# Sixteen-head attentions of a two-layer kernel: masked keys instead of masked queries, score matmuls of 32 rows and 512 columns in pairs of row strips, probability copies shared by two engines

## Chip, cores and metric

One core of a Trainium2 chip runs the whole program. The metric is the device time of one execution in microseconds (us), the median of several runs. The engines are PE (TensorE: matmuls and transposes; PEld is its weight load), DVE (VectorE), ACT (ScalarE), POOL (GpSimd) and SP (SyncE, which issues the DMAs). Every engine works through its own list of instructions in the order of the program, and waits on semaphores for the others.

## The reference

Six stages are added one after another to x, which has 4 batch elements of 128 tokens by 128 channels. Each stage reads the layer norm of x:

```python
x = x + _L0_xattn_ref(_layernorm(x), ctx_1024, ctx_1024, Wq, bq, Wk, bk, Wv, bv, Wo, bo)   # 16 heads, 2048 keys
x = x + _L0_attn_ref(_layernorm(x), ...)      # a state-space scan (conv, 16 states, gate)
x = x + _L0_ffn_ref(_layernorm(x), ...)       # quantised SwiGLU
x = x + _L1_xattn_ref(_layernorm(x), ctx_1024, Wg, bg, Wo, bo)   # gated attention, one head, 2048 keys
x = x + _L1_attn_ref(_layernorm(x), w_qkv, w_proj, b_proj, rel_bias_table)   # 16 heads, 128 keys
x = x + _L1_ffn_ref(_layernorm(x), ...)       # quantised MLP
```

The change is in the two attentions with 16 heads of 8 channels:

```python
# first: a head sees only the keys whose index, less the head's, is a multiple of 16: 128 of the 2048
scores = einsum('bhqd,bhkd->bhqk', Q, K) / sqrt(HEAD_DIM)
scores = where((kidx - hoff) % 16 != 0, -inf, scores)
out = softmax(scores) @ V            # then @ Wo.T + bo
# second: all 128 tokens are keys, and a bias by relative position is added
scores = einsum('bhqd,bhkd->bhqk', q, k) * scale + compute_bias(N, N, rel_bias_table)
```

## The kernel before

Everything between the stages stays in SBUF, with tokens or channels on the 128 partitions. `attention(ph)` is written once for each engine and called for the first (ph 0) and the second (ph 1) 16-head attention. It runs over steps t. A step w from 0 to 15 of an attention handles one batch element b = w // 4 and one group g = w % 4 of four heads, whose 32 channels are partitions 32g to 32g+31. These four steps of a batch element are called a block here.

One step goes through these operations: four score matmuls of 128 queries by 128 keys into one PSUM bank (PE); the negated row maxima (DVE, L753; in the second attention the bias is added by the same instruction, L758); four exponentials with row sums (ACT, L477); four transposes of the probabilities on PE (L1189); and the copy of the transposed probabilities to SBUF (DVE, L775). Transposes and copy of step w come two steps later (LAG = 2), in banks 3 and 4 in turn. Scores use banks 0 to 2 in turn.

Once for each block come: keys and values of the next block (ph 0: two times 16 matmuls into 32-partition column strips, from the transposed context); the placing of values for each head in `v_heads` (L698); `inv_sum`, its transpose (L1204) and its spread over channels; 16 matmuls of values and probabilities (`pv`); `o_T` (ACT, L488); the scaling `attn_T` (L784); the output projection `proj`; the addition to x (L790); and the moments, `rstd` and normalised `xn` for the next layer norm. The constants INVERSE to TURN say how many steps after its block's first step each of these stands. `turn_xn` transposes `xn` for the next stage, and CHANNELS says at which steps the state-space stage's convolution and gate matmuls stand in PE's list. `reduce_weight`, `weight_sums` and `weight_inverses` (from t = WEIGHTS) prepare the scales of the quantised weights.

To keep heads apart, `queries` (L730, L733) writes `q_heads`, four copies of the queries each masked to one head of the group, and the keys are copied by ACT (L427, L459) into `k_groups`, which is zero outside the group's 32 partitions. A score matmul thus reads all 128 partitions of both.

In the second attention `self_queries_keys` makes queries and keys of batch elements 0 to 2 at once and of element 3 later, `self_values` the values. The helper `mm` issues every matmul, at L1076. An f32 matmul shows as two MATMUL records in the trace, a transpose as one.

## Time and profile before

| | us |
|---|---|
| median of 3 runs (lowest, highest) | 281.3 (279.96, 281.42) |
| span of the profiled execution | 278.8 |
| PE busy | 209.7 (75%) |
| DVE busy | 205.7 (74%) |
| ACT busy | 151.6 (54%) |
| POOL busy | 74.6 (27%) |

The span runs from the first to the last instruction; a run's time also holds what lies around it, and differs from one execution to the next. In the trace the first 16-head attention fills the time from 15.56 us (first scores) to about 70 us. The state-space scan follows to 141 us, the SwiGLU to about 165 us, the gated attention to 208 us, and the second 16-head attention runs from 211.0 us (first scores) to 252.9 us (the addition for the last batch element). The rest is the last MLP. A record's time is from its start to its end, and records of one engine overlap, so the distance from one start to the next is often shorter than a record. "PEclk" is the granted TensorE clock as a share of full speed: 1.00 is 2.4 GHz, 0.50 is 1.2 GHz.

### The profile page before, as it was taken

How to read it: one execution, taken by the hardware profiler on the slowest of the kernel's cores; microseconds unless marked ns; L12 is line 12 of the kernel's file. 1: busy time of each engine (PE TensorE's matmuls, PEld its weight loads, DVE VectorE, ACT ScalarE, POOL GpSimd, SP SyncE). 2: the span in 40 equal slices, each digit the busy share in tenths (PEclk: the TensorE clock that was granted, in tenths of full speed). 3: DMA queues.
4: the chain of work that ended last, by engine and by line, in shares of the span. 5: the costliest groups of instructions: out<-in, count | busy, mean ns of one | idle time of the engine just before them, and what ended most of it. 6: DMA issues, size and time to landing. Idle time of an engine off the chain costs nothing.

```text
span 278.8 us, 4790 instructions
## 1 busy us (share of the span) xinstructions
PE 209.7 (75%) x1557; PEld 141.2 (51%) x1559; DVE 205.7 (74%) x585; ACT 151.6 (54%) x510; POOL 74.6 (27%) x73
## 2 busy tenths in 40 slices
PE   6896988898786977777762577999996699973313
PEld 4475877676752322222131354777785688851102
DVE  6358648873069999999957975767767499985675
ACT  4357659643685555555317773245336689853420
POOL 5013000049305777777794010000001000001000
PEclk9688999999979799999996899999999899997555
DMA  7999700068830000000000005000000000000001
GB/s 225 429 393 414 317 2 2 0 74 93 94 45 0 1 0 1 0 0 0 2 1 0 1 0 150 2 0 2 0 1 0 4 1 2 0 4 0 4 0 38
DMA packets 6745, 16.06 MB, mean 58 GB/s; under 512 B 320, under 2 KB 5056, under 8 KB 5696
## 3 DMA queue, kind: packets, MB, share of 16 engines
q1 hardware_dynamic: 6720, 15.75, 19.7%
q8 instruction: 13, 0.21, 0.3%
q14 instruction: 12, 0.10, 0.1%
HBM read 13.39 MB, written 2.35 MB: 56 GB/s over the span
## 4 chain that ended last, share of the span: by engine, by line
PE 38%; DVE 24%; POOL 13%; issue 12%; ACT 9%; DMA 2%; POOLq 0%; SPq 0%; another core or an unknown queue 0%; DVEq 0%; ACTq 0%
PE bank L1076 31%; POOL region L392 13%; ACT probs L477 3%; PE bank L1416 3%; DVE region L775 2%; DVE region L758 2%; DMA ctx_T_sb<-ctx_T 2%; PE bank L1189 2%; DVE neg_max L753 1%; DVE xn L685 1%; DVE stats L680 1%; PE bank L1093 1%; DVE ext L1040 1%; DVE ext L1041 1%; DVE v_heads L698 1%
## 5 line engine op out<-in xcount | busy, mean ns | idle before, releaser
L1076 PE MATMUL bank<-region,early_sb 128*128 128x512 f32 x64 | 36.8, 661 | 11.8 <-POOL region L392 11.6
L392 POOL TENSOR_TENSOR region<-region 128x512 f32<-128x512 f32 x32 | 40.5, 1268 | 14.5 <-DVE region L900 14.5
L900 DVE TENSOR_TENSOR_SCAN region<-region,bank 128x512 f32<-128x512 f32 x32 | 38.7, 1211 | 0.0
L1076 PE MATMUL bank<-k_groups,region 128*128 128x128 f32 x256 | 35.7, 285 | 1.2 <-ACT k_groups L459 1.2
L1076 PEld LDWEIGHTS bank<-k_groups,region 128*128 128x128 f32 x256 | 32.2, 198 | 3.2 <-ACT k_groups L459 1.8
L361 POOL TENSOR_TENSOR xb<-x,rows_sb 128x512 f32<-128x512 f32 x3 | 3.8, 1261 | 101.0 <-DVE x L790 43.2
L477 ACT ACTIVATE probs<-bank,neg_max 128x128 f32<-128x128 f32 x64 | 22.6, 367 | 12.9 <-DVE neg_max L753 12.5
L1076 PE MATMUL bank<-ctx_T_sb,region 128*32 128x128 f32 (+1 forms) x288 | 26.8, 345 | 3.4 <-DMA ctx_T_sb<-ctx_T 2.2
L477 ACT ACTIVATE probs<-region,neg_max 128x128 f32<-128x128 f32 x64 | 24.9, 390 | 5.7 <-DVE neg_max L758 5.5
L1076 PEld LDWEIGHTS bank<-region,early_sb 128*128 128x128 f32 x64 | 10.1, 195 | 33.2 <-POOL region L392 32.6
L775 DVE COPY region<-bank 128x512 f32<-128x512 f32 x32 | 21.8, 682 | 5.6 <-PE bank L1189 5.6
L411 ACT ACTIVATE lnv<-mv,eps_col 128x1 f32<-128x1 f32 x24 | 7.0, 291 | 33.7 <-DVE mv L681 33.6
L542 ACT ACTIVATE region<-bank 128x512 f32<-128x512 f32 x16 | 9.5, 595 | 24.2 <-POOL region L392 24.2
L1189 PE MATMUL bank<-early_sb,probs 128*128 128x128 f32 x128 | 20.7, 287 | 1.5 <-ACT probs L477 1.5
L884 DVE TENSOR_TENSOR bank<-region,bank 128x512 f32<-128x512 f32 x32 | 21.6, 676 | 0.0
L556 ACT ACTIVATE region<-region,a_neg 128x508 f32<-128x508 f32 x32 | 21.1, 708 | 0.0
L758 DVE CUSTOM_DVE_ANT_0 region<-bank,region 128x128 f32<-128x128 f32 x64 | 14.5, 282 | 5.7 <-PE bank L1076 5.7
L1189 PEld LDWEIGHTS bank<-early_sb,probs 128*128 128x128 f32 x128 | 15.2, 146 | 3.5 <-ACT probs L477 2.1
L1007 DVE COPY region<-bank 128x512 f32<-128x512 f32 x16 | 10.9, 686 | 8.1 <-PE bank L1416 8.1
L1076 PEld LDWEIGHTS bank<-region,ctx_sb 128*128 128x128 f32 x128 | 15.4, 192 | 2.9 <-issue 2.9
L1076 PEld LDWEIGHTS bank<-ctx_T_sb,region 128*32 128x32 f32 (+1 forms) x288 | 12.6, 132 | 7.7 <-issue 4.5
L1076 PE MATMUL bank<-region,ctx_sb 128*128 128x128 f32 x128 | 15.6, 275 | 0.0
(198 smaller groups left out, 410.1 us busy)
## 6 DMA issues: line engine op xcount, KB each, us to landing
ctx_sb<-ctx SPq DMA_DIRECT2D x4, 1024.0 KB, 24.5
ctx_T_sb<-ctx_T SPq DMA_DIRECT2D x3, 1024.0 KB, 10.5
late_sb<-late SPq DMA_DIRECT2D x1, 2416.0 KB, 18.4
bias_scratch<-bias_vec SPq DMA_DIRECT2D x1, 2040.0 KB, 24.7
ctx_T_sb<-ctx_T SPq DMA_DIRECT2D x2, 512.0 KB, 6.2
region<-bias_scratch SPq DMA_DIRECT2D x1, 1024.0 KB, 5.7
early_sb<-early SPq DMA_DIRECT2D x1, 512.0 KB, 3.7
region<-taps SPq DMA_DIRECT2D x1, 512.0 KB, 18.9
```

Source lines behind the costliest of these rows:

```text
L392: done(pool.tensor_tensor(read[:, k % 3, :], state[:, k % 3, :], c_sb[:, n % 2, :], ALU.mult), "read")
L477: ins = act.activation(probs[:, w % 4, j, :], src[:, j, :], ACT.Exp, bias=neg_max[:, w % 4, j:j + 1], scale=1.0 if ph == 0 else -1.0, accu ...
L542: done(act.activation(c_sb[:, n % 2, :], bank[2][:, :], ACT.Copy), "c_sb")
L556: done(act.activation(dst, src, ACT.Exp, scale=a_neg[:, hf, n:n + 1]), "decay")
L758: ins = dve.tensor_tensor_reduce(neg_biased[:, t % 3, j, :], src[:, j, :], rel_bias[:, HG * g + j, :], -1.0, HIGHEST, ALU.add, ALU.min, ne ...
L775: done(dve.tensor_copy(probs_T[:, w % (2 * NG)].rearrange("p h k -> p (h k)"), bank[3 + w % 2][:, :]), "probs_T_sb")
L884: done(dve.tensor_tensor(bank[3 + k % 3][:, :], du[:, hf, :], bank[n % 2][:, :], ALU.mult), "drive")
L900: done(dve.tensor_tensor_scan(state[:, k % 3, :], decay[:, k % NDA, :], bank[3 + k % 3][:, :], 0.0, ALU.mult, ALU.add), "state")
L1007: done(dve.tensor_copy(p2_T[:, w % 4].rearrange("p c q -> p (c q)"), bank[4 + w % 2][:, :]), "p2T_sb")
L1076: return pe.matmul(dst, lhsT, rhs, start=start, stop=stop)
L1189: ins = pe.transpose(bank[3 + w % 2][:, j * P:j * P + P], probs[:, w % 4, j, :], ident)
L1416: ins = pe.transpose(bank[4 + w % 2][:, c * P:c * P + P], p2[:, b % 2, g, c * P:c * P + P], ident)
```

## The change

The mask moves from the queries to the keys. `q_sb` holds the queries once (scaled by 8 ** -0.5), and `k_exp[:, b, j, :]` holds the keys of a batch element four times, each with only the channels of head j of every group. A score step is then one matmul of 32 partitions (a row strip of TensorE) by 512 columns. Steps are issued in pairs, (t+2, t+3) at every even t, two row strips into two of four banks. Keys of the first attention come from the 16 matmuls with `wz` without accumulation, into four column ranges of bank 6, and DVE adds the masked bias; in the second, four matmuls with `wkz` (the key weights masked for each head, made by POOL) and one ACT copy. All transposes go to bank 4, one step after the exponentials; DVE copies the even steps and ACT the odd ones. The stages of a block come two to four steps earlier, and the convolution matmuls stand elsewhere.

```diff
-LAG = 2
-INVERSE, INVERSE_T, VALUES, SCALE, PROJECT, ADD, RSTD, NORM, TURN = 6, 7, 8, 9, 10, 11, 11, 12, 13
+INVERSE, INVERSE_T, VALUES, HEADS_OUT, SCALE, PROJECT, ADD, RSTD, NORM = 4, 5, 5, 6, 7, 7, 8, 8, 9
+STEPS = 23
-WEIGHTS = 9
-LAST_TURN, LAST_QK = 2, 6
-CHANNELS = {17: [(0, 0)], 18: [(0, 1)], 23: [(0, "gates"), (1, "gates")], 25: [(1, 0), (1, 1)]}
+WEIGHTS = 6
+LAST_TURN, LAST_QK = 2, 3
+TURNS = {13: 0, 15: 1, 18: 2, 22: 3}
+CHANNELS = {16: [(0, 0), (0, 1)], 17: [(0, "gates")], 19: [(1, 0), (1, 1), (1, "gates")]}
...
+            for j in range(HG):
+                done(pool.tensor_copy(wkz[:, j, :, j, :],
+                                      L("wqkvT")[:, D:2 * D].rearrange("p (g k d) -> p g k d", g=NG, k=HG)[:, :, j, :]),
+                     "wkz")
...
             def self_keys(b):
-                act.wait_ge(S["kv_ps"], 2 * NB + 1 + b // (NB - 1))
-                for g in range(NG):
-                    rows = slice(32 * g, 32 * g + 32)
-                    ins = act.activation(k_groups[rows, g, b * P:b * P + P], bank[6][rows, b * P:b * P + P], ACT.Copy)
-                done(ins, "k_sb")
+                act.wait_ge(S["k_ps"], NB + b + 1)
+                done(act.activation(k_exp[:, b, :, :].rearrange("p j k -> p (j k)"), bank[6][:, :], ACT.Copy), "k_sb")
+
+            def turned_probs(w):
+                act.wait_ge(S["probs_T_ps"], w + 1)
+                if w // NG >= 2:
+                    act.wait_ge(S["pv"], w // NG - 1)
+                done(act.activation(probs_T[:, w % (2 * NG)].rearrange("p h k -> p (h k)"), bank[4][:, :], ACT.Copy),
+                     "probs_T_sb")
...
+                    if 0 <= t - 1 < 4 * NB and (t - 1) % 2:
+                        turned_probs(ph * 16 + t - 1)
...
+            def keys(v):
+
+                dve.wait_ge(S["k_ps"], v + 1)
+                done(dve.tensor_tensor(k_exp[:, v, :, :], bank[6][:, :].rearrange("p (j k) -> p j k", j=HG),
+                                       bk_heads[:, :, None].to_broadcast([P, HG, P]), ALU.add), "k_sb")
...
+                maxima(ph, 0)
+                for t in range(STEPS):
+                    if ph == 0 and ahead(t, 1) is not None:
+                        keys(ahead(t, 1))
+                    if t + 1 < 4 * NB:
+                        maxima(ph, t + 1)
+                    if 0 <= t - 1 < 4 * NB and (t - 1) % 2 == 0:
+                        w = ph * 16 + t - 1
                         dve.wait_ge(S["probs_T_ps"], w + 1)
...
+            def score(ph, t):
+                b, g = t // NG, t % NG
+                rows = slice(32 * g, 32 * g + 32)
+                pe.wait_ge(S["k_sb"], ph * NB + b + 1)
+                pe.wait_ge(S["q_sb"], 1 if ph == 0 else 2 + b // (NB - 1))
+                if t >= 4:
+
+                    pe.wait_ge(S["probs" if ph == 0 else "neg_max"], ph * 16 + t - 3)
+                done(mm(bank[t % 4][:, :], q_sb[rows, b * P:b * P + P],
+                        k_exp[rows, b, :, :].rearrange("p j k -> p (j k)")), "scores")
...
+                score(ph, 0)
+                score(ph, 1)
+                for t in range(STEPS):
+                    if t % 2 == 0 and t + 2 < 4 * NB:
+                        score(ph, t + 2)
+                        score(ph, t + 3)
+                    if ahead(t, 0) is not None:
+                        (keys if ph == 0 else self_keys)(ahead(t, 0))
+                    if ph == 0 and ahead(t, 1) is not None:
+                        values(ahead(t, 1))
+                    if 0 <= t - 1 < 4 * NB:
+                        w = ph * 16 + t - 1
+                        pe.wait_ge(S["probs"], w + 1)
+                        if w >= 1:
+                            pe.wait_ge(S["probs_T_sb"], w)
...
-                            ins = pe.transpose(bank[3 + w % 2][:, j * P:j * P + P], probs[:, w % 4, j, :], ident)
+                            ins = pe.transpose(bank[4][:, j * P:j * P + P], probs[:, w % 4, j, :], ident)
...
                     if ph == 1 and t == LAST_QK:
-                        self_queries_keys(NB - 1, NB)
-                    if ph == 1 and t == LAST_TURN + 1:
+                        self_queries(NB - 1, NB)
                         self_values()
```

`ahead(t, phase)` is the batch element b from 1 to 3 for which t = 4(b-1) + phase.

How PE's list changes in the first attention, where `L1076` and `L1101` are `mm`, `L1189` and `L1243` the transposes of probabilities, `ctx_T_sb` the keys or values of the next batch element and `v_heads` the `pv` matmuls. Before, from the scores of step 10 on:

```order
L1076 MATMUL bank2<-k_groups,region 128x128 x4
L1189 MATMUL bank4<-early_sb,probs 128x128 x4
L1117 MATMUL bank6<-early_sb,v_T 128x128
L1204 MATMUL bank7<-early_sb,inv_sum 16x128
L1076 MATMUL bank0<-k_groups,region 128x128 x4
L1189 MATMUL bank3<-early_sb,probs 128x128 x4
L1076 MATMUL bank5<-region,v_heads 32x128 x16
L1076 MATMUL bank7<-inv_T,cols_sb 128x128
```

And now, from the pair of steps 10 and 11 on:

```order
L1101 MATMUL bank2<-k_exp,region 128x512
L1101 MATMUL bank3<-k_exp,region 128x512
L1101 MATMUL bank6<-ctx_T_sb,region 32x128 x16
L1243 MATMUL bank4<-early_sb,probs 128x128 x4
L1101 MATMUL bank5<-ctx_T_sb,region 32x128 x16
L1243 MATMUL bank4<-early_sb,probs 128x128 x4
L1254 MATMUL bank7<-early_sb,inv_sum 16x128
L1101 MATMUL bank5<-region,v_heads 32x128 x16
L1101 MATMUL bank7<-inv_T,cols_sb 128x128
L1101 MATMUL bank0<-k_exp,region 128x512
L1101 MATMUL bank1<-k_exp,region 128x512
```

Eight score matmuls of two steps became two, keys and values stand around one set of transposes, and `pv` stands three steps earlier, ahead of the next pair of scores.

How ACT's list changes in the second attention, from the copy of the keys of batch element 2 on. Before:

```order
L459 ACTIVATE k_groups<-bank6 32x128 x4
L477 ACTIVATE probs,row_sum<-region,neg_max 128x128 x12
L459 ACTIVATE k_groups<-bank6 32x128 x4
L477 ACTIVATE probs,row_sum<-region,neg_max 128x128 x4
L488 ACTIVATE o_T<-bank5 128x128
L477 ACTIVATE probs,row_sum<-region,neg_max 128x128 x12
```

And now (`L472` is the copy of transposed probabilities):

```order
L466 ACTIVATE k_exp<-bank6 128x512
L490 ACTIVATE probs,row_sum<-region,neg_max 128x128 x8
L472 ACTIVATE region<-bank4 128x512
L503 ACTIVATE o_T<-bank5 128x128
L490 ACTIVATE probs,row_sum<-region,neg_max 128x128 x8
L472 ACTIVATE region<-bank4 128x512
L430 ACTIVATE lnv<-mv,eps_col 128x1
L431 ACTIVATE rstd<-lnv 128x1
L466 ACTIVATE k_exp<-bank6 128x512
L490 ACTIVATE probs,row_sum<-region,neg_max 128x128 x8
```

After every second step's exponentials ACT has a copy of 512 columns, and the four key copies of a batch element became one.

## Rows read from the trace of the kernel before

**Rows 1.** The page: chain of work that ended last, share of the span by line.

```profile
PE bank L1076 31%; POOL region L392 13%; ACT probs L477 3%; PE bank L1416 3%; DVE region L775 2%; DVE region L758 2%; DMA ctx_T_sb<-ctx_T 2%; PE bank L1189 2%; DVE neg_max L753 1%; DVE xn L685 1%; DVE stats L680 1%; PE bank L1093 1%; DVE ext L1040 1%; DVE ext L1041 1%; DVE v_heads L698 1%
```

**Rows 2.** Busy us (instructions) of each engine by stretch; granted clock; DMA share, GB/s.

```profile
40.00:50.00 10.00, 8.83 (x120) 7.74 (x119) 7.84 (x21) 6.58 (x32) 0.00 (x0) 1.00 0.01 2
237.00:247.00 10.00, 9.13 (x118) 7.90 (x121) 9.83 (x57) 9.28 (x48) 0.00 (x0) 1.00 0.00 0
```

**Rows 3.** PE's timeline, first attention: start, us to the last end, operation, shape, count.

```profile
15.56 1.06 PE L1076 MATMUL bank<-k_groups,region 128*128 128x128 f32 x8
...
31.63 1.06 PE L1076 MATMUL bank<-k_groups,region 128*128 128x128 f32 x8
32.53 0.60 PE L1189 MATMUL bank<-early_sb,probs 128*128 128x128 f32 x4
...
36.96 1.08 PE L1076 MATMUL bank<-ctx_T_sb,region 128*32 128x128 f32 x32
37.97 0.66 PE L1189 MATMUL bank<-early_sb,probs 128*128 128x128 f32 x4
38.56 1.08 PE L1076 MATMUL bank<-region,v_heads 128*32 128x128 f32 x32
39.57 0.48 PE L1076 MATMUL bank<-inv_T,cols_sb 16*128 16x128 f32 x2
```

**Rows 4.** The chain in order of time: a 512-column f32 matmul of the gated attention.

```profile
174.74 0.86 PE bank L1076 x2
```

**Rows 5.** Groups by shape, 9 to 70 us: count, busy us, mean ns, idle before.

```profile
L477 ACT ACTIVATE probs<-bank,neg_max 128x128 f32<-128x128 f32 x64 | 22.6, 367 | 12.9 <-DVE neg_max L753 12.5
L753 DVE TENSOR_REDUCE neg_max<-bank 128x4 f32<-128x512 f32 x16 | 10.9, 684 | 5.2 <-PE bank L1076 5.0
L775 DVE COPY region<-bank 128x512 f32<-128x512 f32 x16 | 10.9, 682 | 5.6 <-PE bank L1189 5.6
L427 ACT ACTIVATE k_groups<-bank,cols_sb 32x128 f32<-32x128 f32 x16 | 5.7, 355 | 0.2
L730 DVE TENSOR_SCALAR region<-bank,cols_sb 128x128 f32<-128x128 f32 x16 | 5.4, 402 | 4.7 <-PE bank L1076 4.7
```

**Rows 6.** The page: an ACT copy of 512 columns out of PSUM, in the scan.

```profile
L542 ACT ACTIVATE region<-bank 128x512 f32<-128x512 f32 x16 | 9.5, 595 | 24.2 <-POOL region L392 24.2
```

**Rows 7.** Busy time and granted clock, as rows 2, around two slow stretches.

```profile
22.40:25.70 3.30, 1.44 (x11) 1.09 (x9) 3.30 (x9) 3.16 (x17) 1.14 (x2) 1.00 1.03 431
25.80:29.10 3.30, 2.76 (x36) 2.28 (x37) 1.08 (x6) 1.50 (x8) 1.53 (x3) 0.50 1.00 420
217.00:220.20 3.20, 0.76 (x7) 0.68 (x7) 2.14 (x11) 3.14 (x16) 0.00 (x0) 1.00 0.00 0
220.40:223.60 3.20, 3.20 (x17) 3.20 (x17) 0.94 (x9) 0.61 (x4) 0.00 (x0) 0.50 0.01 3
```

**Rows 8.** ACT's and PE's timelines: last exponentials and last convolution, first attention.

```profile
57.37 0.37 ACT L477 ACTIVATE probs<-bank,neg_max 128x128 f32<-128x128 f32 x1 [1.02 <-DVE neg_max L753]
...
58.41 0.37 ACT L477 ACTIVATE probs<-bank,neg_max 128x128 f32<-128x128 f32 x1
...
68.91 0.20 ACT L412 ACTIVATE rstd<-lnv 128x1 f32<-128x1 f32 x1
...
69.73 3.75 PE L1076 MATMUL bank<-region 128*128 128x128 f32 x32
```

**Rows 9.** ACT's and DVE's timelines: last exponentials and last addition, second attention.

```profile
245.34 0.40 ACT L477 ACTIVATE probs<-region,neg_max 128x128 f32<-128x128 f32 x1
...
246.51 0.39 ACT L477 ACTIVATE probs<-region,neg_max 128x128 f32<-128x128 f32 x1
...
252.90 0.29 DVE L790 TENSOR_TENSOR x<-bank,xb 128x128 f32<-128x128 f32 x1 [0.58 <-PE bank L1076]
```

More of the change, by code:

```diff
@@ L1154, in self_queries_keys, with self_keys @@
                 if b0:
[L1156 to L1157 removed]
+                    pe.wait_ge(S["q_sb"], 2)
                 done(mm(bank[5][:, cols], L("wqkvT")[:, 0:D], xn_T[:, cols]), "q_ps")
[L1159 removed]
+            def self_keys(b):
+                pe.wait_ge(S["xnT_sb"], 3 * NB + b + 1)
+                pe.wait_ge(S["wkz"], HG)
+                if b:
+                    pe.wait_ge(S["k_sb"], NB + b)
+                for j in range(HG):
+                    ins = mm(bank[6][:, j * P:j * P + P], wkz[:, j].rearrange("p g k d -> p (g k d)"),
+                             xn_T[:, b * P:b * P + P])
+                done(ins, "k_ps")
             def self_values():
```

246 lines of the change are left out of this document (119 added, 127 removed).

## The prediction

> **What bounds the kernel now.** I read the chain of waits first. Its largest share, 31%, lies on PE's matmuls of `mm` [rows 1], which stand for several stages, so I read the busy time by stretch next, for the two stages that change. In the first attention PE is busy 8.83 of 10 us, DVE 7.84 and ACT 6.58: PE's list is nearly full [rows 2]. In the second DVE is busy 9.83 of 10 us and ACT 9.28, PE 9.13: all three are full and DVE leads [rows 2]. So a microsecond taken from PE counts in the first attention, and one taken from DVE in the second, until ACT is the bound, which has only half a microsecond in ten to give there. Everything from the scan to the gated attention is unchanged and starts when the first attention ends; the last MLP starts when the second ends. The sum is therefore the shift of two ends.
>
> **Prices.** Four score matmuls of 128 columns take PE 0.90 us (31.63 to 32.53) [rows 3]. One f32 matmul of 512 columns takes 0.86 us by itself [rows 4]. So a step alone gains nothing; the gain is that two row strips run side by side. No row here shows row strips. The nearest is the column strips: 32 records of 128 columns in 1.01 us (36.96 to 37.97), 32 ns each, where records of the full array take 0.90/8 = 113 ns [rows 3]. Side by side a pair costs 0.86 us, one after another 1.72. I take the first, being the nearest row in kind. Changing between full array and strips costs about 0.15 us: transposes take 0.44 us before a like shape, but 0.59 ahead of `v_heads` (37.97 to 38.56) [rows 3]. Half of it shows for a pair, so I use 0.95 us for a pair against 1.80 before.
>
> The Trainium skill (TensorE: Matmul & The Clock Gate, Part 3, packing small matmuls) gives a speed-up of 3.07 for four row strips of 512 columns, short of 4; by that a pair would be an estimated 1.1 us, and ten pairs on the path would add 1.5 us to the sum. The same skill (TensorEngine Tiling, Tiling Modes) says that a change of tiling mode drains TensorE, which speaks against this change, for it makes 16 more such switches in each direction; the trace agrees with a drain, with the 0.15 us above.
>
> DVE loses eight copies of 0.60 us start to start (0.68 each by itself) in each attention, and in the first also 16 masked queries (402 ns) for one pass over 512 columns, and gains four key additions of about 0.68 [rows 5]. ACT loses 16 key copies of 355 ns in the first attention [rows 5] and gains eight probability copies. A 512-column ACT copy out of PSUM is 595 ns [rows 6], about 0.50 when the next follows at once. The exponentials of a step keep ACT for 1.39 us in the first attention (57.37 to 58.41 is three of four) [rows 8] and for 1.56 in the second [rows 9].
>
> **First attention.** The first scores stand behind the transpose of the values as before, at 15.5 us [rows 3]; the smaller `q_sb` write is hidden there. Then a block repeats. I count from the end of the exponentials of step 4b-1:
>
> - PE: pair 0.95, keys 1.01, transposes of step 4b-1 landing after 0.66 [rows 3]: 2.6 us. ACT had finished the next exponentials at 1.4 and waits 1.2 us for this copy. That is a new wait: keys are queued ahead of the transposes.
> - PE goes on: values to 3.4, transposes 4b to 3.9, `inv_sum` 0.1, `pv` 1.01, spread 0.41, the next pair 0.95, transposes 4b+1 landing: 7.0.
> - ACT: copy 0.5, `v_T` and `o_T` 0.5, exponentials 4b+3 1.5: 9.5. About nine hand-overs of 0.04 us make it 9.85 us.
>
> Before, 15 steps passed from 15.56 to 57.37, 2.79 each, 11.1 us for a block [rows 3, 8]. Now the start-up to the end of exponentials 3 takes 8.7 us: two pairs and the keys 2.9, key addition and maxima 1.4, exponentials 2 1.4, then the wait for transposes 1, copy 0.5, `v_T` 0.3 and exponentials 3 1.5. Two blocks take 19.7. The last, without keys and values but with the weight sums, takes 8.2. The exponentials of step 15 then start at 52.1, 5.2 us earlier.
>
> The tail gives some back. The convolution of the first two batch elements (3.7 us) stands ahead of the last `pv`, as before. But half of the 3.75 us of last convolutions [rows 8], with its gates 2.3 us, now stands ahead of the last projection instead of behind it. I get the last `rstd` at 65.2 where it ended at 69.1 [rows 8], 3.9 earlier; the work behind it is shorter by the moved part, but ACT needs its table load and the activations of the others first. What reaches the scan is **-4.1 us**. POOL's quantised weights come earlier and are not waited for; its `wkz` copies (about 0.6 us) stand ahead of `w_tap`, which is used 25 us later.
>
> **Second attention.** Score matmuls wait only for DVE's maxima here, so a pair is issued early. But the copies of odd steps now stand in ACT's list, the one with least room. Its work up to the exponentials of step 15: 15 steps of 1.55 is 23.3, seven copies 3.5, three key copies 1.5, `xn_T` and `o_T` 0.8, two `rstd` 1.0, in all 30.1 us. From 212.8, where the first exponentials start (0.35 earlier than before through the shorter key copy), that gives 242.9 with no wait at all. ACT will wait, though: for transposes 3, behind the late queries, values and a pair (1.1 us); for transposes 5, behind `pv`, which waits for the 16 value placements on DVE (2.5 us); for transposes 7, behind a projection, a pair and keys (1.2 us); and 0.3 for transposes 11. So step 15 starts at 248.0, against 245.34 [rows 9]: 2.6 later. The shorter lags save 2.0 behind it: from the start of step 15 to the last addition were 7.56 us [rows 9], and are now 1.7 for the exponentials, 0.65 and 0.6 for transposes and copy, and 2.6 from `pv` on. Net **+0.6 us**.
>
> **The clock.** The granted clock fell to 0.50 for 3.3 us after PE had been busy 1.44 of 3.30 us, and once more after 0.76 of 3.20 [rows 7]. Both prices above are at 1.00. The new first attention has the same kind of thin stretch at about 21.7 to 24.2 us (1.0 us busy or less), the second at about 214 to 218.6 (2.0 of 5). Right behind each stand a pair, keys and transposes that ACT waits for, so a slow stretch costs up to 1.7 us. I count one of two: **+1.7 us**.
>
> **The sum** is -4.1 + 0.6 + 1.7 = -1.8 us on a span of 278.8, so 277.0. The profiled span lies 2.5 us under the median, 281.3, and I leave that distance: **279.5 us**.
>
> **Rivals.**
>
> 1. *The two strips of a pair run one after another.* For it: no row shows two row strips together, and each f32 matmul is two passes. Against: the column strips, whose f32 matmuls are two passes too. Price 0.86 us for every pair that the path passes. It passes about five of eight in each attention, so +8.6 us, 288.1. Half an overlap (1.29 for a pair) gives 283.8. It is slower than before as soon as a pair costs over 1.15 us.
> 2. *The clock falls in most blocks.* PE's blocks get emptier: between transposes 4b+1 and the next pair it has 0.8 us of work in 2.8. Two more slow stretches on the path add 3.4 us: 282.9.
> 3. *ACT is the bound in the first attention as well, and the waits for transposes disappear.* If PE runs ahead of my list, ACT needs 5.6 + 1.0 + 0.5 + 0.5 = 7.6 us for a block instead of 9.85. Two blocks and half the waits of the second attention give 4.5 us more: 275.0.
> 4. *The moved copies only change places:* DVE's gain is ACT's loss and the end stays. With a first attention that gains 2 and a second that loses 2 it is 281.3.
>
> **How the numbers follow.** Chances: the forecast 0.50 (276 to 282 with its clock and half a microsecond for each hand-over sum), rival 1 0.20, rival 2 0.13, rival 3 0.09, rival 4 0.08. The range 275.5 to 287 leaves out most of a full rival 1 and the lower end of rival 3. A measurement of this kernel tells about 0.5% from no change, 279.9 to 282.7. Faster than that: 0.35 of the forecast's 0.50, all of rival 3, together 0.44. Within: 0.12 of the forecast, rival 4, half of rival 2: 0.25. Slower: rival 1, half of rival 2, the rest: 0.31.
>
> **What would show it.** In the profile of the changed kernel: the two score matmuls of a pair start within some 10 ns and the pair's last end is 1.0 us behind its start (rival 1: 1.3 or 1.8). ACT's idle time ahead of the copies of odd steps is released by PE's transposes, over 1 us in each block of the first attention. The exponentials of step 15 start near 52 and 248 us less the shift of the first attention. In the second attention DVE is no longer full and ACT is the busiest. The granted clock has at most three slow stretches in both. I would be wrong from the start if the first scores came late, for the 512-column key addition now stands between keys and scores, or if the step from one block to the next were under 9 us.

## The result, and the profile after

The changed kernel takes **307.7 us** (median of 4 runs, 306.9 to 308.0) where the kernel before takes 280.95 (4 runs, 279.96 to 281.42): a ratio of **1.095, 95% interval 1.092 to 1.098**. The forecast was 279.5 us with a range up to 287. It was wrong in sign and by far in size. The profiled execution spans 306.1 us against 278.8, and its mean granted clock is 0.788 against 0.907. Ratios, here and below, leave out executions over 1.5% above the fastest of their kernel; medians and ranges hold all.

Nearly all of the 27.3 us lies in the two attentions. From the first scores to the last addition, or `rstd`, of each, the windows view of the changed kernel gives (columns as in [rows 2]: length, then busy us and instructions of PE, PEld, DVE, ACT, POOL, then the granted clock):

```profile
15.40:79.00 63.60, 55.09 (x489) 36.04 (x489) 29.36 (x81) 30.96 (x154) 17.02 (x18) 0.73 0.57 148
221.20:280.30 59.10, 46.22 (x279) 29.10 (x279) 28.36 (x184) 32.87 (x150) 0.00 (x0) 0.62 0.00 1
```

And the same two of the kernel before:

```profile
15.60:68.90 53.30, 45.99 (x570) 38.82 (x569) 36.13 (x98) 32.12 (x159) 13.09 (x13) 0.97 0.52 158
211.00:252.90 41.90, 35.05 (x353) 30.48 (x353) 34.76 (x202) 31.48 (x151) 0.00 (x0) 0.96 0.01 2
```

Three things are to be seen. The stages grew by 10.3 and 17.2 us. PE has 81 and 74 instructions fewer and is busy 9 and 11 us longer. And the clock, which was at full speed but for one short stretch in each stage, is now 0.73 and 0.62 in the mean. DVE lost 6.8 and 6.4 us of work; ACT's stayed within 1.4.

The page of the changed kernel, waits for the turned probabilities first (DVE's copy L788, ACT's copy L472), then the scores:

```profile
L788 DVE COPY region<-bank 128x512 f32<-128x512 f32 x16 | 11.1, 691 | 30.8 <-PE bank L1243 30.8
L472 ACT ACTIVATE region<-bank 128x512 f32<-128x512 f32 x16 | 9.5, 597 | 38.0 <-PE bank L1243 38.0
L1101 PE MATMUL bank<-k_exp,region 32*128 32x512 f32 x64 | 25.2, 882 | 0.7 <-ACT k_exp L466 0.7
```

Both engines that were to share the copies stand idle for PE's transposes, 30.8 and 38.0 us over the two attentions. Before, DVE's copies waited 5.6 us in the first [rows 5] and 0.1 in the second. The chain of waits still has PE's `mm` at the top, 33% of the span after 31% [rows 1]:

```profile
PE bank L1101 33%; POOL region L411 13%; PE bank L1243 7%; PE bank L1471 2%; ACT region L472 2%; ACT probs L490 2%; DVE ext L1065 1%; DVE ext L1066 1%; DVE xn L697 1%; DVE region L972 1%; DVE stats L692 1%; DVE region L1080 1%; DVE h_abs L941 1%; DVE attn_T L804 1%; ACT region L595 1%
```

The transposes (L1243, 7% where L1189 had 2%) rose most. One block of the first attention in PE's timeline, at full clock:

```profile
44.42 1.08 PE L1101 MATMUL bank<-region,v_heads 128*32 128x128 f32 x32
45.61 0.48 PE L1101 MATMUL bank<-inv_T,cols_sb 16*128 16x128 f32 x2
45.84 1.12 PE L1101 MATMUL bank<-k_exp,region 32*128 32x512 f32 x4
46.89 0.66 PE L1243 MATMUL bank<-early_sb,probs 128*128 128x128 f32 x4
48.32 0.63 PE L1243 MATMUL bank<-early_sb,probs 128*128 128x128 f32 x4 [0.78 <-ACT region L472]
49.93 0.71 PE L1101 MATMUL bank<-cols_sb,attn_T 128*128 128x128 f32 x2 [0.98 <-DVE attn_T L804]
```

A pair of score matmuls (four records, since each f32 matmul is two) keeps PE for 1.05 us, 45.84 to 46.89. So the two strips do run side by side. But behind them come gaps, and then the clock falls. The windows view around three of the slow stretches:

```profile
33.00:36.30 3.30, 1.67 (x11) 0.84 (x8) 1.67 (x5) 2.22 (x11) 0.00 (x0) 1.00 0.11 45
36.40:43.20 6.80, 6.77 (x63) 4.07 (x67) 4.26 (x13) 2.27 (x12) 0.00 (x0) 0.50 0.01 4
46.70:49.90 3.20, 1.47 (x10) 0.84 (x8) 2.12 (x5) 2.32 (x12) 0.00 (x0) 1.00 0.00 0
50.00:60.00 10.00, 9.73 (x58) 5.64 (x59) 5.44 (x20) 3.77 (x19) 3.48 (x3) 0.50 0.50 56
247.00:258.00 11.00, 9.24 (x58) 6.10 (x59) 5.85 (x34) 6.29 (x31) 0.00 (x0) 0.50 0.01 2
```

From 50 to 60 us PE is the engine that all others wait for (9.73 of 10 us busy) and runs at 1.2 GHz. ACT's timeline in that stretch shows the price, one wait of 4 us ahead of a copy:

```profile
55.35 0.60 ACT L472 ACTIVATE region<-bank 128x512 f32<-128x512 f32 x1 [3.96 <-PE bank L1243]
```

**A first estimate of the clock's share.** With only two levels of clock, a mean clock c over a span s means (1 - c)/0.5 x s at half clock: 130 us in the changed kernel, 52 before, other stages included. So 78 us more at half clock go with 27.3 us more of span, 0.35 us for each. Whether that is cause or by-product is what the experiments are for.

### The profile page after: what moved, and what is told of

It reads as the page before. It is cut to its first block, busy times and chain, and to the rows that moved or that the text cites. A ratio compares the mean times of both kernels' runs of the same rounds, so it can differ in the third digit from the quotient of the medians.

```text
span 306.1 us, 4414 instructions
## 1 busy us (share of the span) xinstructions
PE 231.1 (75%) x1393; PEld 137.8 (45%) x1395; DVE 190.6 (62%) x544; ACT 150.1 (49%) x498; POOL 75.9 (25%) x78
## 4 chain that ended last, share of the span: by engine, by line
PE 43%; POOL 13%; DVE 13%; issue 9%; ACT 8%; POOLq 0%; another core or an unknown queue 0%; DVEq 0%; ACTq 0%
PE bank L1101 33%; POOL region L411 13%; PE bank L1243 7%; PE bank L1471 2%; ACT region L472 2%; ACT probs L490 2%; DVE ext L1065 1%; DVE ext L1066 1%; DVE xn L697 1%; DVE region L972 1%; DVE stats L692 1%; DVE region L1080 1%; DVE h_abs L941 1%; DVE attn_T L804 1%; ACT region L595 1%
## 5 line engine op out<-in xcount | busy, mean ns | idle before, releaser
L1101 PE MATMUL bank<-region,early_sb 128*128 128x512 f32 x64 | 35.9, 643 | 11.7 <-POOL region L411 11.6
L1243 PE MATMUL bank<-early_sb,probs 128*128 128x128 f32 x128 | 28.7, 365 | 11.6 <-ACT region L472 10.0
L1243 PEld LDWEIGHTS bank<-early_sb,probs 128*128 128x128 f32 x128 | 19.5, 185 | 25.2 <-issue 16.9
L1101 PE MATMUL bank<-ctx_T_sb,region 128*32 128x128 f32 (+1 forms) x288 | 28.8, 387 | 2.3 <-DMA ctx_T_sb<-ctx_T 1.9
L788 DVE COPY region<-bank 128x512 f32<-128x512 f32 x16 | 11.1, 691 | 30.8 <-PE bank L1243 30.8
L472 ACT ACTIVATE region<-bank 128x512 f32<-128x512 f32 x16 | 9.5, 597 | 38.0 <-PE bank L1243 38.0
L376 POOL TENSOR_TENSOR xb<-x,rows_sb 128x512 f32<-128x512 f32 x2 | 2.5, 1264 | 101.5 <-DVE x L812 60.2
L1101 PE MATMUL bank<-k_exp,region 32*128 32x512 f32 x64 | 25.2, 882 | 0.7 <-ACT k_exp L466 0.7
L1101 PEld LDWEIGHTS bank<-region,early_sb 128*128 128x128 f32 x64 | 9.6, 188 | 33.4 <-POOL region L411 33.1
L554 ACT ACTIVATE region<-bank 128x512 f32<-128x512 f32 x16 | 9.5, 595 | 24.2 <-POOL region L411 24.2
L1101 PEld LDWEIGHTS bank<-ctx_T_sb,region 128*32 128x32 f32 (+1 forms) x288 | 14.5, 152 | 10.7 <-issue 8.8
L1101 PEld LDWEIGHTS bank<-region,ctx_sb 128*128 128x128 f32 x128 | 15.4, 192 | 2.9 <-issue 2.9
L1032 DVE COPY region<-bank 128x512 f32<-128x512 f32 x16 | 10.9, 685 | 8.1 <-PE bank L1471 8.1
L1101 PE MATMUL bank<-region 128*128 128x128 f32 (+2 forms) x52 | 14.8, 459 | 1.2 <-ACT region L438 1.2
## 6 DMA issues: line engine op xcount, KB each, us to landing
ctx_T_sb<-ctx_T SPq DMA_DIRECT2D x3, 1024.0 KB, 10.3
region<-taps SPq DMA_DIRECT2D x1, 512.0 KB, 20.3
```

What stands on the lines that cost most here:

```text
L472: done(act.activation(probs_T[:, w % (2 * NG)].rearrange("p h k -> p (h k)"), bank[4][:, :], ACT.Copy), "probs_T_sb")
L554: done(act.activation(c_sb[:, n % 2, :], bank[2][:, :], ACT.Copy), "c_sb")
L788: done(dve.tensor_copy(probs_T[:, w % (2 * NG)].rearrange("p h k -> p (h k)"), bank[4][:, :]), "probs_T_sb")
L1032: done(dve.tensor_copy(p2_T[:, w % 4].rearrange("p c q -> p (c q)"), bank[4 + w % 2][:, :]), "p2T_sb")
L1101: return pe.matmul(dst, lhsT, rhs, start=start, stop=stop)
L1243: ins = pe.transpose(bank[4][:, j * P:j * P + P], probs[:, w % 4, j, :], ident)
```

## The experiments

The theories: **A**, the halved clock takes the time, and waits matter only because they let it fall. **B**, the new waits take it themselves (one bank for transposes, ScalarE's copies behind its exponentials, keys ahead of transposes), the clock is a by-product. And on why the clock falls: **C**, matmuls on 32 rows hold it up less than matmuls on 128, whatever PE's busy time says; **D**, only idle time counts.

| kernel | median us | range (runs) | ratio to before (95%) | clock |
|---|---|---|---|---|
| changed | 307.7 | 306.9-308.0 (4) | 1.095 (1.092-1.098) | 0.788 |
| e1_fill | 287.4 | 285.6-288.3 (4) | 1.019 (1.013-1.026) | 0.883 |
| e2_all_rows | 301.2 | 300.7-302.2 (4) | 1.069 (1.064-1.075) | 0.866 |
| e3_before_strips | 299.8 | 299.2-304.8 (4) | 1.063 (1.057-1.070) | 0.828 |
| e4_keys_behind | 292.4 | 290.5-301.5 (4) | 1.034 (1.025-1.043) | 0.842 |
| e5_fill_behind | 286.7 | 284.3-288.1 (4) | 1.023 (1.010-1.035) | 0.891 |
| e6_dve_copies | 292.8 | 291.9-293.3 (4) | 1.046 (1.037-1.054) | 0.905 |
| e7_before_fill | 280.8 | 279.9-283.2 (10) | 1.004 (1.000-1.009) | 0.918 |
| e8_thin_fill | 292.5 | 289.8-304.3 (4) | 1.042 (1.030-1.053) | 0.878 |
| e9_fill_small | 282.2 | 279.7-285.4 (10) | 1.008 (1.003-1.014) | 0.904 |
| e10_fill_project | 291.1 | 284.9-294.4 (4) | too scattered for one | 0.868 |
| e11_all_rows_behind | 296.5 | 294.8-299.2 (4) | 1.057 (1.049-1.065) | 0.880 |
| e12_thin_small | 301.3 | 289.1-304.9 (6) | too scattered for one | 0.869 |

The clock is the mean of the profiled execution. The kernel before had 280.5 to 281.4 us beside them.

**Idle time filled.** e1_fill adds bf16 matmuls of 128 rows by 256 columns, with a result that nobody reads. `keep_warm(n, at)` issues n of them into bank `at`; FILL_A is 6, FILL_B is 8. Such matmuls are called fillers here:

```diff
                         pe.wait_ge(S["probs"], w + 1)
+                        if t % 2 and t < 4 * NB:
+                            keep_warm(FILL_A, (t - 1) % 4)
                         if w >= 1:
...
                         v = ph * NB + due(t, PROJECT)
+                        if t < 4 * NB:
+                            keep_warm(FILL_B, (t - 1) % 4)
                         pe.wait_ge(S["attn"], v + 1)
```

> The changed kernel with idle-time matmuls added on TensorE in both attentions: 6 bf16 products of 128 rows ahead of the transposes of odd steps (behind the wait on the probabilities) and 8 ahead of each projection's wait, into a score bank that is free. Their results are overwritten; nothing else changes. Theory A (most of the loss is the halved clock, and the waits are only what lets it fall): the mean granted clock of both attentions goes from about 0.6 to over 0.95 and the time falls from 307.7 to about 280-286 us, although PE has more to do. Theory B (the new dependency waits cost the time themselves, the clock is a by-product): the clock may rise, but the time stays over 300 us, or rises.

287.4 us, 20.3 us less although PE got more to do: 1.4 above theory A's band, 13 below theory B's. Theory B is out as the main cause, since no dependency was removed. The first attention of e1_fill, as above, is back at its old clock, the second nearly so:

```profile
15.40:69.60 54.20, 50.05 (x562) 35.36 (x561) 29.09 (x81) 31.43 (x156) 17.07 (x18) 0.97 0.65 171
213.20:260.50 47.30, 40.82 (x351) 27.54 (x351) 27.77 (x184) 32.89 (x150) 0.00 (x0) 0.92 0.01 2
```

**Rows, in the changed kernel.** e2_all_rows leaves out the separation of the four groups, so its result is not the reference's; it is there for its time:

```diff
-                b, g = t // NG, t % NG
-                rows = slice(32 * g, 32 * g + 32)
+                b = t // NG
+                rows = slice(0, P)
```

> The changed kernel with its score matmuls over all 128 partitions instead of the group's 32. The scores then sum over all four groups (this changes the computation), the number of instructions, their order and all waits stay. The two matmuls of a pair can then no longer run side by side: a pair takes about 1.72 us instead of about 1.05 at full clock, 5 us more of PE's work in each attention. Theory C (the clock falls because 32-row strips use a quarter or half of the array): the clock falls in fewer stretches and the time is lower than the changed kernel's 307.7, about 288-298 us, though PE has more work. Theory D (the clock falls for idle gaps alone, whatever the rows): idle gaps shrink by 0.7 us a pair, clock changes little, and the time is 307 to 316 us. Clearly lower than 300 us is C's, over 307 is D's.

301.2 us, between the two bands: 6.5 us faster than with strips, although pairs can't overlap any more. A pair now takes 1.82 us at full clock (37.24 to 39.06), 0.77 more than two strips, some 12 us for 16 pairs. Its clock, 0.866, means 50 us less at half clock, an estimated 18 us at the 0.37 found below; the difference is near what was measured. The sign is C's, the size is under what I gave it. By itself the run doesn't exclude D, for the longer pairs also fill gaps.

**Rows, in the kernel before.** e3_before_strips keeps everything of the kernel before and narrows its scores to the 32 rows that hold data:

```diff
-                                     q_heads[:, j, b * P:b * P + P], k_groups[:, g, b * P:b * P + P])
+                                     q_heads[32 * g:32 * g + 32, j, b * P:b * P + P],
+                                     k_groups[32 * g:32 * g + 32, g, b * P:b * P + P])
```

> The kernel before with one edit: each score matmul reads only the group's 32 partitions (the left-out ones are zero, so nothing else changes); still four matmuls of 128 columns a step, still in the same place and order. Theory C (thin rows let the clock fall): the granted clock of the first attention (15.5 to 69 us), which has been 1.00 but for one stretch, falls to 0.50 in several stretches, and the time rises from 281 to 286-300 us. Theory D (idle gaps alone): PE's busy time in microseconds and its gaps stay as they were, the clock too, and the time is within 0.5% of 281.

**299.8 us, 6.3% slower, from rows alone.** It is the cleanest run of the study: same list, same order, same waits, and the same data but for zeros. Both kernels lose their clock near 25 us. With full rows it is back after 3.3 us [rows 7]; with strips it stays down for 10.3 us in which PE has no gap. Then a stretch in which PE is busy 3.08 of 3.40 us is followed by half clock, and from 222.6 the clock stays down for 27 us:

```profile
24.60:34.90 10.30, 10.30 (x92) 8.23 (x92) 4.26 (x12) 5.12 (x26) 2.78 (x4) 0.50 0.83 343
34.90:38.30 3.40, 3.08 (x23) 2.43 (x22) 2.54 (x6) 2.01 (x11) 0.00 (x0) 1.00 0.01 2
38.30:45.10 6.80, 6.71 (x70) 5.20 (x74) 2.47 (x8) 2.87 (x16) 0.00 (x0) 0.50 0.01 2
222.60:249.90 27.30, 26.06 (x135) 21.35 (x131) 17.45 (x109) 18.00 (x85) 0.00 (x0) 0.50 0.01 2
```

What PE did in the second of these, by its timeline (15 of the 23 records are 32-row scores):

```profile
34.70 1.02 PE L1076 MATMUL bank<-k_groups,region 32*128 32x128 f32 x7
35.65 0.66 PE L1190 MATMUL bank<-early_sb,probs 128*128 128x128 f32 x4
36.24 1.15 PE L1076 MATMUL bank<-k_groups,region 32*128 32x128 f32 x8
37.32 0.66 PE L1190 MATMUL bank<-early_sb,probs 128*128 128x128 f32 x4
```

The kernel before has a stretch with much less work, all on 128 rows but for two small records, and keeps its clock behind it:

```profile
49.60:53.00 3.40, 2.17 (x20) 1.84 (x16) 3.40 (x8) 2.75 (x16) 0.00 (x0) 1.00 0.00 0
53.00:56.40 3.40, 3.40 (x28) 2.83 (x28) 2.49 (x8) 2.10 (x12) 0.00 (x0) 1.00 0.01 2
```

Theory D can't have both.

A rival has to be weighed: changing between the full array and strips costs PE time too. At full clock a step's scores and transposes take 1.67 us here (47.57 to 49.24) and 1.33 before (32.53 to 33.86). But the exponentials of steps 10 to 13 start 7.04 us apart in both kernels (50.37 to 57.41 here, 44.89 to 51.93 before), each at full clock, so in the first attention that time is hidden. In the second, steps 10 to 15 take 9.92 us at full clock against 9.34, which for a whole attention would be an estimated 2 of the 18 us. So most of the loss came through the clock.

**The order of PE's list.** e4_keys_behind moves four lines of `attention` behind the transposes:

```diff
-                    if ahead(t, 0) is not None:
-                        (keys if ph == 0 else self_keys)(ahead(t, 0))
-                    if ph == 0 and ahead(t, 1) is not None:
-                        values(ahead(t, 1))
                     if 0 <= t - 1 < 4 * NB:
...
                         done(ins, "probs_T_ps")
+                    if ahead(t, 0) is not None:
+                        (keys if ph == 0 else self_keys)(ahead(t, 0))
+                    if ph == 0 and ahead(t, 1) is not None:
+                        values(ahead(t, 1))
```

> The changed kernel with the matmuls of keys and values (512 and 128 columns) moved on PE from ahead of a step's transposes to behind them, so that ScalarE's copy of the turned probabilities and the exponentials behind it wait less. Theory B (the order of PE's list and the waits it makes cost the time): three blocks of each attention lose about 1 us each, some 5 us in all, 302 us or less. Theory A (the halved clock costs the time): the same work at the same clock with the gap in another place, 305 to 310 us; a large move in either direction only where the clock's slow stretches move too.

292.4 us, three times what B gave it, and the clock rose to 0.842 (one of the four executions took 301.5 us, at 0.809). By the expectation's last clause that is a move of the slow stretches: half clock falls from 130 to 92 us, 38 less for 15.4 us of span. Which of the two it was, the next run tells.

**Both edits.** e5_fill_behind has the edits of e1 and e4.

> The changed kernel with both earlier edits: the idle-time matmuls (6 ahead of the transposes of odd steps, 8 ahead of each projection's wait) and the matmuls of keys and values behind a step's transposes. If halved clock and wait order are two causes that add, each takes what the other leaves: the clock is at 1.00 in nearly all of both attentions, and the blocks lose another 0.5 to 1 us each on top of the 287.4 us of the fillers alone: 279-284 us. If moving the keys helped only because it filled a thin stretch (clock 0.84 instead of 0.79), there is nothing left for it to give at full clock: 286-289 us.

286.7 us, within the scatter of e1's 287.4. Beside these fillers the order of keys and transposes is worth under a microsecond, so nearly all of its 15 us in e4 came through the clock. But PE was now full of fillers, which can hide a shorter wait; no run has small groups in the first order. A group of six stands between two groups of transposes and keeps PE for 0.85 us, 43.90 to 44.75:

```profile
43.41 0.66 PE L1243 MATMUL bank<-early_sb,probs 128*128 128x128 f32 x4
43.90 0.82 PE L1103 MATMUL bank<-ones 128*128 128x256 bf16 x6
44.75 0.33 PE L1243 MATMUL bank<-early_sb,probs 128*128 128x128 f32 x1
```

**ScalarE's half of the copies.** e6_dve_copies undoes it on top of e5:

```diff
                 act.wait_ge(S["vT_ps"], v + 1)
+                if v >= 2:
+                    act.wait_ge(S["pv"], v - 1)
...
-                    if 0 <= t - 1 < 4 * NB and (t - 1) % 2:
-                        turned_probs(ph * 16 + t - 1)
...
-                    if 0 <= t - 1 < 4 * NB and (t - 1) % 2 == 0:
+                    if 0 <= t - 1 < 4 * NB:
```

> The kernel with both of those edits, and with all copies of the turned probabilities on VectorE again, none on ScalarE (one wait on pv is added for ScalarE's copy of the values, for the bank it reads). It undoes the change's last part at a clock that is held up. If the ScalarE copies are a cost (they stand behind a step's exponentials, in the list of the engine with least room), it is 2-4 us faster than the kernel with both edits; if VectorE is the one that needed relief (9.83 of 10 us busy in the second attention before), it is 2-5 us slower. My own forecast: first attention a little faster, second slower, within 1.5 us in all.

292.8 us, 6.1 slower than e5. The clock is not the reason: from 216 to 252 us in e5 and from 219 to 255 in e6 it is 0.91, in the first attentions 0.97. (The higher mean of the profiled execution, 0.905, comes mostly from the first 15 us.) My own forecast, within 1.5 us, missed. Sharing the copies is the part of the change that pays, in this order of work.

**Fillers in the kernel before.** e7_before_fill:

```diff
                     if ph == 0 and t % NG == 3 and t // NG + 1 < NB:
+                        if t == 3:
+                            keep_warm(12, (t - 2) % 3)
                         turn_values(t // NG + 1)
...
                     if ph == 1 and t == LAST_QK:
+                        keep_warm(18, (t - 2) % 3)
                         self_queries_keys(NB - 1, NB)
```

> The kernel before with idle-time matmuls in two places where TensorE waits ahead of a slow stretch: 12 ahead of the first transpose of the values in the first attention (22.6 to 24.2 us), 18 ahead of the late queries of the second (217.1 to 219.5 us). Theory A (half clock costs in proportion to PE's work on the path): both slow stretches of 3.4 us go and the time falls by 1 to 2.5 us, to 279-280 us. If the waits hide the half clock: within 0.3% of before.

280.8 us, a ratio of 1.004 (1.000 to 1.009): no gain. But the run tests less than it was meant to. The slow stretch of the first attention is gone; that of the second came all the same:

```profile
218.40:221.70 3.30, 0.85 (x7) 0.61 (x6) 2.38 (x13) 3.23 (x16) 0.00 (x0) 0.99 0.00 0
221.80:225.10 3.30, 3.30 (x17) 3.30 (x17) 0.52 (x5) 0.84 (x5) 0.00 (x0) 0.50 0.01 2
```

The 18 fillers stand in the wrong place. PE's wait in the first row is 2.45 us ahead of the values (`self_values`, 221.17). The late queries, with the fillers ahead of them, come at t = 6, and the fillers run from 227.79 to 229.76, behind the slow stretch and where PE had no wait. So one short stretch was removed and 2 us of work was added elsewhere. What a single short stretch costs stays open.

**Fillers on 32 rows.** e8_thin_fill is e1_fill with the same number, place and columns of fillers:

```diff
+            def keep_thin(n, at):
+                rows = slice(32 * at, 32 * at + 32)
+                for _ in range(n):
+                    mm(bank[at][:, 0:2 * P], ones[rows, :].bitcast(BF16)[:, 0:P], ones[rows, :].bitcast(BF16))
```

> The changed kernel with the same idle-time matmuls as in the first filler run, in the same number, places and columns, but over 32 rows instead of 128. TensorE's busy time is the same as in that run. Theory C (thin rows do not hold the clock up): the clock stays near the changed kernel's 0.79 in the mean and the time at 303-310 us. Theory D (only busy or idle counts): as with full-row fillers, 287 us.

292.5 us (289.8 to 304.3): worse than with full rows (287.4), far better than none, so neither theory's number. Thin fillers hold the clock up too, only less: one slow stretch of the first attention is 17.1 us long, where e1 has some 11 us at half clock in both attentions together (0.97 of 54.2 us, 0.92 of 47.3). The two mean clocks, 0.878 and 0.883, hide that, for they hold all other stages. Its windows view has, in one execution, both halves of the argument:

```profile
45.20:48.60 3.40, 3.40 (x22) 1.69 (x22) 1.82 (x7) 2.51 (x15) 0.00 (x0) 1.00 0.00 0
48.70:65.80 17.10, 16.18 (x87) 11.33 (x87) 6.41 (x23) 7.37 (x34) 12.35 (x9) 0.50 0.80 89
233.10:236.40 3.30, 1.65 (x38) 1.27 (x37) 2.20 (x15) 3.30 (x17) 0.00 (x0) 1.00 0.01 2
236.50:239.80 3.30, 3.30 (x29) 1.86 (x22) 1.22 (x12) 1.31 (x6) 0.00 (x0) 1.00 0.00 0
```

PE is busy without a gap from 45.2 to 48.6, mostly on fillers and scores of 32 rows, and the clock halves for 17 us. From 233.1 it is busy for half of the time, on transposes and `pv` (128 rows), and the clock stays.

**Fewer fillers.** e9_fill_small is e5 with groups of 3 and 4 instead of 6 and 8.

> The changed kernel with keys and values behind the transposes and half the idle-time matmuls: 3 ahead of the transposes of odd steps, 4 ahead of each projection's wait (6 and 8 gave 286.7 us at a clock of 0.891). In that run TensorE had next to no idle time left in the attentions, and each group of 6 stood 0.66 us between two groups of transposes. If the fillers themselves cost what remains above the kernel before, and half of them still hold the clock at 1.00: 282-284 us. If half of them let the clock fall again: 288-292 us. If the new order costs the rest (a wait for ScalarE's copy in each odd step): 286-287 us as before.

**282.2 us, the best of the changed kernels**, as expected if the fillers themselves cost what was left: 25.5 of the 26.7 us are back, for 10 fillers in a block. The two stages, as above:

```profile
15.40:68.90 53.50, 46.70 (x526) 31.40 (x525) 29.27 (x81) 31.43 (x156) 17.06 (x18) 0.97 0.65 173
209.70:253.50 43.80, 35.12 (x315) 23.20 (x315) 27.77 (x183) 32.99 (x150) 0.00 (x0) 0.96 0.01 2
```

Beside the rows of before at the top: same clocks, 0.97 and 0.96, and stages of 53.5 and 43.8 us against 53.3 and 41.9. That is as near as these runs come to the change with the clock taken out; keys and values stand behind the transposes here, and each attention has 36 fillers.

**Only around the projections.** e10_fill_project is e5 with the 8 ahead of the projections alone.

> The same order with idle-time matmuls only ahead of the projections, 8 each, three groups in each attention. In the run with keys and values behind the transposes and no fillers, the four falls of the clock inside the attentions came after stretches of 3.4 us with 1.64, 1.64, 1.65 and 2.26 us of PE's work, each around a projection. If those stretches are what lets the clock fall, six groups are enough: the clock holds in both attentions and the time is 280-283 us, the best of the changed kernels. If not, 288-292 us.

291.1 us; missed, and its fastest execution, 284.9, is outside the first band too. The clock did hold from 32 to 70 us, where those projections are, but fell at 25.6 and 223.6 in the starts of the attentions, where e9 has groups of 3. Covering the stretches after which it had fallen doesn't do.

**All rows in the better order.** e11_all_rows_behind joins e2 and e4; like e2 it leaves out the separation of the groups.

> The changed kernel with keys and values behind the transposes and score matmuls over all 128 partitions (which changes the computation: scores sum over all four groups), no idle-time matmuls. Theory C (32-row strips leave the array too thin for the clock): the clock is above the 0.84 of the same order with strips and the time is no worse than its 292.4 us although a pair takes 1.72 us instead of 1.05; 284-291 us. Theory E (the all-row run of before gained only through shorter idle gaps, which this order has closed already): slower than 292.4, 294-300 us.

296.5 us, theory E's number: the clock is higher than e4's (0.880 against 0.842) and the time is 4.1 us longer. So strips have two sides that nearly balance: they save PE's time on a pair and cost clock. In the first order 128 rows win by 6.5 us, in this one strips by 4.1.

**Thin fillers, few.** e12_thin_small is e9 with the 32-row fillers of e8.

> The kernel with keys and values behind the transposes and the small groups of idle-time matmuls (3 and 4), which gave 282.2 us at a clock of 0.904, with those matmuls over 32 rows instead of 128: same number, columns, places and busy time. The thin fillers in the first order came out at 292.5 us where full ones gave 287.4, between the two theories. Theory C (32-row work holds the clock up less than 128-row work): with this little filler the difference decides in more stretches, the clock falls in at least two more of them inside the attentions, mean below 0.88, time 286-292 us. Theory D (thin and full rows count alike): 282 us, within 0.7%.

Median 301.3 us, worse than either theory. Its six executions lie between 289.1, inside C's band, and 304.9; the fastest is slower than the slowest of e9's ten, 285.4. With each one's own mean clock: 289.1 at 0.869, 293.8 at 0.853, 300.7 at 0.821, 301.9 at 0.840, 304.8 at 0.812, 304.9 at 0.806. Between the ends that is 42 us more at half clock for 15.9 us of time. It differs from e9 in nothing but the rows of the fillers. In the profiled, fastest execution a stretch and its sequel read

```profile
44.80:48.20 3.40, 2.96 (x17) 1.32 (x18) 1.83 (x7) 2.50 (x15) 0.00 (x0) 1.00 0.02 5
48.20:55.00 6.80, 6.80 (x53) 4.87 (x53) 4.35 (x17) 2.70 (x13) 4.28 (x4) 0.50 0.75 84
```

and in e9_fill_small, at the same place,

```profile
44.80:48.20 3.40, 2.86 (x17) 1.46 (x16) 1.86 (x7) 2.07 (x12) 0.00 (x0) 1.00 0.02 5
48.20:55.00 6.80, 4.74 (x56) 3.13 (x55) 3.98 (x16) 4.96 (x24) 4.71 (x4) 1.00 0.80 89
```

Less busy, more rows, full clock behind it. The two stretches differ little (some thin fillers here, three more transposes there), so the times and clocks of all executions weigh more than this pair. C stands, as a matter of degree.

**The price of half clock**, estimated from pairs of executions: changed to e9, 76 us less at half clock for 26.7 us of span, 0.35 for each; changed to e4, 0.41; before to e3, 50 us for 18.6, 0.37; within e12, 0.37. Only the last pair has no other difference; changed to e1, where much work was added, gives 0.31. The Trainium skill (TensorE: Matmul & The Clock Gate, HAM oscillation) counts half of the throttled time as lost, 0.5 for each. These runs stay under that; that PE is not the bound in all of it is the likely reason, and not tested. The Trainium skill (the same page, Part 1) ties the clock to how busy PE has been; in e3 and e8 busy time alone doesn't tell it.

## Why the prediction was wrong, step by step

- **The clock step failed.** It read "I count one of two: +1.7 us", that is some 3 us more at half clock. It was 78 us more. The price in it was not the fault: 1.7 us for a stretch of 3.3 is 0.5, over the 0.37 of the runs. The count was. I looked for thin stretches by PE's busy time, as in [rows 7], and took the score matmuls as holding the clock like any other. They are the very work that the change thins: from 128 rows to 32, and by overlap from 1.80 us of a pair to 1.05. By e3 the first of these alone costs the kernel before 18 us, an estimated 2 of them by dearer switches. The sign named for this step, at most three slow stretches in both attentions, was missed too: there were seven.
- **Rival 2** had the mechanism, "the clock falls in most blocks", and priced it at two more stretches, 282.9 us. What it lacked is that one fall leads to the next. From 50.0 to 70.5 and from 241.2 to 258.3 the clock stayed down: a slower PE keeps ACT waiting, and its own next work comes later. That link is argued from the timeline; no run isolates it.
- **A pair of strips** was right: 0.95 us forecast, 1.05 measured, not 1.72. Rival 1 is out. The estimate that stood beside it, 1.1, from the Trainium skill (TensorE: Matmul & The Clock Gate, Part 3), was the nearer one.
- **ACT's waits for transposes** were right in place (all behind L1243) and too small: 16.6 us in the first attention, where the list had a little over 1.2 in each of its blocks. At half clock the transposes and the keys ahead of them take nearly double (keys 1.87 us in the changed kernel, 39.37 to 41.24, for 1.01). But even in e9, with the clock held, ACT waits 9.7 us for them, so the term was too low by itself.
- **The blocks of the first attention**: 9.85 us forecast; 11.4, 13.5 and 14.1 measured (starts of exponentials 3, 7, 11, 15 at 23.6, 35.0, 48.5, 62.6). In e9, with the clock held and ten fillers in each, they are 10.2, 10.5 and 10.7, so the list itself was nearly right. Step 15 came at 62.6 instead of 52.1, in e9 at 54.7. The sum has a slip here: it counts from the end of exponentials 3, so 52.1 is by its own count the end of step 15's and not the start, 1.4 us of difference.
- **The tail** gave back more than I said. Of the 2.7 us that e9 is ahead at step 15 (54.7 against 57.4) nothing is left at the last `rstd`, 68.89 against 68.91. I had it give back 1.3 of 5.2. The place is the one that the prediction named, between the last `pv` and the last projection. These are the rows, e9_fill_small first:

```profile
61.90 1.08 PE L1103 MATMUL bank<-region,v_heads 128*32 128x128 f32 x32
...
63.32 1.13 PE L1103 MATMUL bank<-region,late_sb 128*128 128x256 f32 x4
...
64.93 2.05 PE L1103 MATMUL bank<-region 128*128 128x128 f32 x16 [0.37 <-ACT region L440]
66.82 0.61 PE L1103 MATMUL bank<-region,late_sb 128*128 128x128 f32 x4
67.27 0.39 PE L1103 MATMUL bank<-cols_sb,attn_T 128*128 128x128 f32 x2
...
68.89 0.20 ACT L433 ACTIVATE rstd<-lnv 128x1 f32<-128x1 f32 x1
```

  and the kernel before:

```profile
65.25 1.08 PE L1076 MATMUL bank<-region,v_heads 128*32 128x128 f32 x32 [0.36 <-DVE x L790]
...
67.19 0.49 PE L1076 MATMUL bank<-cols_sb,attn_T 128*128 128x128 f32 x2 [0.18 <-DVE attn_T L784]
```

  In e9 `pv` starts 3.35 us earlier and the projection 0.08 later. Its `attn_T` is ready at 63.8, but gates, convolution and gates stand ahead of it in PE's list, 3.95 us (63.32 to 67.27) where the prediction had 2.3. In the changed kernel the distance from `pv` to projection is the same, 5.37 us (72.02 to 77.39), at full clock.
- **The second attention** was forecast to lose 0.6 us; it lost 17.2, and 1.9 in e9. DVE is no longer full, as forecast, and ACT is the busier of the two, but the busiest of all is PE (46.22 of 59.10 us, in e9 35.12 of 43.80). With the clock held the walk through ACT's list came out: from the first exponentials to step 15's are 35.3 us in e9 (211.85 to 247.16), forecast 35.2, against 32.2 before and 49.2 in the changed kernel.
- **Rival 3**, ACT as the bound and the waits gone, is out by the same 16.6 us. Its price had a slip: two blocks at 2.25 us are already the 4.5 that it gives for two blocks and half the waits of the second attention; with those, 5.1 us in all, it would have been 7.0.
- **Rival 4**, "the moved copies only change places", gave 281.3 us, near to e9's 282.2, but by luck: by e6 the move itself is worth 6 us, in the order that the change brought.

With the clock held, in e9, the scan starts 1.0 us earlier than before (84.5 against 85.5) and the last addition of the second attention comes 0.6 later (253.5 against 252.9), fillers included. The sum without its clock term was -3.5 us at that point. If e9 may stand for the change at a held clock, the other terms were 4 us too low in all, 3.1 of them at the start of the scan (-4.1 forecast), most of that in the tail. Still open are why ScalarE's share is worth so much where the whole is worth nothing, and how much of e9's remaining 0.8% is its own fillers. No version found beats the kernel before.

## What to carry to other kernels

Before packing or narrowing matmuls, ask what they do for the clock as well as what they cost: work on 32 rows may fill PE's time and yet let its clock fall, and then every other engine waits. Read the granted clock of each stage first when a kernel comes out slower than its list, and test the clock by a few full-row matmuls in idle time; here groups of six and eight (e1) told cause from by-product. Then look in the trace whether each filler landed in the wait that it was meant for: in e7 18 of 30 did not. Where executions of one kernel scatter by several per cent, look whether their clocks scatter with them.

## What was not expected of the hardware

- PE busy for 3.40 of 3.40 us, mostly on 32-row matmuls, was followed by 17 us at half clock; busy for 1.65 of 3.30 on 128-row work, it kept its clock (e8).
- Narrowing matmuls from 128 rows to 32, with no other edit, cost 6.3% (e3).
- Executions of one kernel differed by 15.9 us, with mean clocks from 0.869 to 0.806 (e12).
- The same walk through the steps takes the same 7.04 us with strips and with full rows when both are at full clock (e3 and before), although PE's part of a step is 0.34 us longer with strips.
- Each microsecond at half clock goes with an estimated 0.31 to 0.41 us of time (e1, e3, e4, e9, e12).
